# Column scans that keep the running line in contiguous buffers and let ScalarE copy it home, with the rows written out in four strips

## The chip, the cores and the metric

One core of a Trainium2 chip. The metric is the device time of one execution in microseconds (us); times of several runs are given as their median. Profiled values come from one execution of the program. The engines are TensorE (PE in the rows, PEld for its weight loads), VectorE (DVE), ScalarE (ACT), GpSimd (POOL) and SyncE (SP), which here only issues transfers.

## The reference

The input is `x` of shape (4, 48, 128, 128) in float32. Four residual layers are applied to it, each to a group-normalised copy:

```python
x = x + _L0_conv_ref(_gn(x), ...)   # 1x1 and 3x3 convolutions, channel attention
x = x + _L1_conv_ref(_gn(x), ...)   # four line scans
x = x + _L2_conv_ref(_gn(x), ...)   # the same with other weights
x = x + _L3_conv_ref(_gn(x), ...)   # gated MLP over tokens
```

A scan layer walks over the image line by line. Every new line is the old content of that line plus a 5-tap convolution of the line that was finished just before, over 48 channels in and out:

```python
def f(carry, inp):
    nxt = inp + _conv1d(carry, w, b)
    return (nxt, nxt)
```

It does so over the rows downwards, over the rows upwards, over the columns to the right and over the columns to the left, 127 steps each. No step can start before the one before it is done. Eight such scans (two layers of four) stand in the program.

## The kernel before

The whole image stays on the chip in `image`, in float32. The 128 partitions hold two halves: 48 channels from partition 0 (`LO`) and 48 from partition 64 (`HI`), for even and odd positions along the line, so that the 5 taps become three products of 112 x 112 weights. The free dimension is `(g s k j b)`: `g` a pair of the four batches and `b` the batch in it, `s` and `k` the row or column index (`s` its parity), `j` the position along a row. `line(g, along_w, at)` gives one line of two batches, 128 numbers in a partition. In a row scan these are one contiguous run of 512 bytes. In a column scan (`along_w`) they are 64 pairs of numbers: 8 bytes each, 512 bytes from one to the next.

One scan step runs the two groups g = 0 and 1 in turn. TensorE makes three products into `bank[g]` (lines 1134 to 1136; each is two instructions with a weight load each), counted by `s_prod[g]`. VectorE adds the old line to the bank and writes the new line into `image` (line 1489), counted by `s_state[g]`, on which TensorE's next step of that group waits. While VectorE adds for one group, TensorE multiplies for the other. In the program's numbering the scans are 0 (down), 1 (up), 2 (right) and 3 (left); `SCANS` holds them, and 2 and 3 are the column scans.

Around the scans:

- During scan 1 ScalarE exchanges the halves of finished rows (`exchange`, three copies for every two steps, in a loop of its own), so that the column scans find their layout. It does nothing in scan 2.
- The layer's input is kept in HBM (`saved`) as 16 tiles, four to each strip of 16 column indices `j` (32 columns). SyncE brings them into six buffers (`bring`) and, in the first scan layer, saves the sums again.
- In scan 3, whenever a half strip (16 columns) is finished, GpSimd adds the kept input to it in the buffer (`add_strips`, four adds for a half strip, waiting for `s_prod`). ScalarE then copies the sums back into `image` (`swap_home` in the first layer, `rows_home` in the second, 8 instructions for a half strip) and counts `s_home`. VectorE takes statistics of what came home (`strip_piece`), one instruction behind each add. There are eight half strips; the last is added by VectorE itself (`add_last`) when the scan has ended.
- In the second scan layer SyncE also writes the finished rows to HBM (`send_rows`, in two halves of the row, for four batches) and reads them back as tokens (`bring_tokens`) for the MLP. `s_flat[b]` counts the rows of batch b. GpSimd and ScalarE wait for `s_flat[1]`, since two of the MLP's buffers lie where batch 1 stood, and TensorE waits for GpSimd's four fills of these buffers (`s_gate_zero`) before it turns the first tokens.

An instruction of these engines carries one wait with it. Where the program puts two waits ahead of an instruction, the instruction carries the first one and the second becomes an instruction of its own that runs ahead of it.

## Time and profile before

| | us |
|---|---|
| median of 3 runs | 2387.31 (2385.31 to 2390.0) |
| the profiled execution | 2381.65 |
| its span, first to last instruction | 2379.8 |
| mean granted clock of TensorE | 0.971 of full speed |

The profiled execution lies 5.66 us under the median of the runs. Its scans stand between 740 and 2140 us of the span: the first layer's from 743 to 1427 us, the second's from 1455 to 2140 us. Before them are the convolutions and the attention, behind them the MLP. A row of the timeline has start and duration in us, engine, line, operation and shapes, and in brackets the idle time ahead of it with what ended it.

### The profile page before, as it was taken

The page shows a single profiled execution, that of the slowest core. Times are in us where ns is not written, and L with a number is a line of the kernel's source. Part 1 is how long each engine was busy: PE and PEld are TensorE (multiplying, and loading weights), DVE is VectorE, ACT ScalarE, POOL GpSimd, SP SyncE. Part 2 cuts the span into 40 slices and gives each one's busy share as a digit, 9 for nine tenths or more (in the row PEclk, how much of TensorE's full clock was granted, in tenths as well). Part 3 has the DMA queues.
Part 4 walks back from the last instruction along what each step waited for, and adds up shares of the span by engine and source line. Part 5 has one row for each costly group of instructions (what it writes and reads, how often), then busy time and mean ns, then how long its engine had stood idle before and what let it go on. Part 6 is the DMA issues. An engine that isn't in the chain of part 4 may idle for free.

```text
span 2379.8 us, 42935 instructions
## 1 busy us (share of the span) xinstructions
PE 2182.0 (92%) x17386; PEld 1969.6 (83%) x17386; DVE 1396.8 (59%) x3514; ACT 761.6 (32%) x1088; POOL 412.7 (17%) x411
## 2 busy tenths in 40 slices
PE   2989999999999999999999995999999999992786
PEld 2889759669536999999999995999999999991554
DVE  5866666766775444444555886444444555884555
ACT  6922342442546002440002347003440001223542
POOL 2233203213104800000003430300000003430200
PEclk9999999999999999999999997999999999996998
DMA  7700111121237940000001531400000000567835
GB/s 128 117 12 11 13 25 16 15 45 37 55 57 145 145 89 2 1 1 1 1 1 40 148 108 54 81 1 2 1 1 1 1 1 18 102 122 202 275 107 159
DMA packets 237974, 139.31 MB, mean 59 GB/s; under 512 B 197728, under 2 KB 222560, under 8 KB 230368
## 3 DMA queue, kind: packets, MB, share of 16 engines
q1 hardware_dynamic: 236640, 135.79, 27.0%
q8 instruction: 136, 2.23, 0.4%
q10 hardware_dynamic: 1024, 0.91, 0.2%
q14 instruction: 46, 0.38, 0.1%
q0 software_dynamic: 128, 0.01, 0.0%
HBM read 77.06 MB, written 62.92 MB: 59 GB/s over the span
## 4 chain that ended last, share of the span: by engine, by line
PE 87%; DVE 7%; ACT 2%; DMA 1%; issue 1%; SPq 1%; POOL 0%; ACTq 0%; DVEq 0%; POOLq 0%
PE bank L1134 20%; PE bank L1135 19%; PE bank L1136 18%; PE bank L1024 10%; PE bank L1095 7%; PE bank L1027 4%; PE bank L1098 2%; DVE work L1412 2%; PE bank L1246 2%; PE bank L1039 1%; PE bank L1173 1%; PE bank L1218 1%; DVE stats L1269 1%; DMA image<-flat_rows 1%; SPq L577 1%
## 5 line engine op out<-in xcount | busy, mean ns | idle before, releaser
L1489 DVE TENSOR_TENSOR image<-bank,image 112x128 f32<-112x128 f32 x2032 | 656.5, 323 | 638.8 <-PE bank L1136 609.3
L1134 PE MATMUL bank<-image,scan_area 112*112 112x128 f32 x4064 | 807.3, 280 | 12.8 <-ACT image L875 6.7
L1135 PE MATMUL bank<-image,scan_area 112*112 112x126 f32 x4064 | 771.2, 271 | 0.0
L1136 PE MATMUL bank<-image,scan_area 112*112 112x126 f32 x4064 | 770.2, 270 | 0.0
L1135 PEld LDWEIGHTS bank<-image,scan_area 112*112 112x112 f32 x4064 | 581.6, 176 | 0.0
L1134 PEld LDWEIGHTS bank<-image,scan_area 112*112 112x112 f32 x4064 | 567.1, 175 | 16.5 <-ACT image L875 7.1
L1136 PEld LDWEIGHTS bank<-image,scan_area 112*112 112x112 f32 x4064 | 578.9, 176 | 0.0
L1024 PE MATMUL bank<-work 128*128 128x192 f32 x1536 | 307.5, 337 | 28.6 <-DVE work L1412 27.2
L372 POOL TENSOR_TENSOR work<-image,work 112x1024 f32<-112x1024 f32 x56 | 129.2, 2337 | 1078.2 <-PE bank L1136 1076.3
L1024 PEld LDWEIGHTS bank<-work 128*128 128x128 f32 x1536 | 249.5, 194 | 34.2 <-issue 33.1
L807 ACT COPY work<-work 32x1008 f32<-32x1008 f32 x128 | 132.0, 1031 | 297.8 <-PE bank L1027 194.7
L1412 DVE COPY work<-work 32x1008 f32<-32x1008 f32 x256 | 208.7, 815 | 4.5
L667 POOL TENSOR_TENSOR band<-band,work 128x384 f32<-128x384 f32 x124 | 145.8, 1176 | 285.2 <-DVE work L1370 285.2
L871 ACT COPY work<-image 48x256 f32 (+1 forms) x128 | 51.5, 403 | 418.1 <-PE bank L1136 417.8
L1095 PE MATMUL bank<-work 128*48 128x512 f32 x768 | 179.7, 602 | 4.0 <-DVE work L1404 4.0
L881 ACT COPY image<-work 48x1024 f32<-48x1024 f32 x64 | 67.1, 1049 | 292.7 <-POOL work L372 282.6
L1027 PE MATMUL bank<-work 96*128 96x96 f32 x1024 | 151.1, 270 | 0.0
L1027 PEld LDWEIGHTS bank<-work 96*128 96x128 f32 x1024 | 150.4, 194 | 0.0
L1095 PEld LDWEIGHTS bank<-work 128*48 128x48 f32 x768 | 51.6, 124 | 115.7 <-issue 111.1
L1367 DVE COPY work<-bank 128x384 f32<-128x384 f32 x128 | 71.3, 557 | 128.2 <-PE bank L1027 126.9
L890 ACT ACTIVATE image<-work,b_col 112x512 f32<-112x512 f32 x64 | 44.7, 777 | 313.6 <-POOL work L372 302.7
L799 ACT ACTIVATE work<-image,gn_shift,gn_scale 112x576 f32<-112x576 f32 (+1 forms) x128 | 110.7, 908 | 2.3 <-DVE gn_shift L1311 0.9
(163 smaller groups left out, 1524.0 us busy)
## 6 DMA issues: line engine op xcount, KB each, us to landing
work<-saved SPq DMA_DIRECT2D x64, 384.0 KB, 8.5
saved<-saved SPq DMA_DIRECT2D x32, 384.0 KB, 7.4
saved<-work SPq DMA_DIRECT2D x32, 384.0 KB, 5.7
flat_rows<-image SPq DMA_DIRECT2D x16, 768.0 KB, 13.1
image<-flat_rows SPq DMA_DIRECT2D x4, 3072.0 KB, 18.1
out<-image SPq DMA_DIRECT2D x8, 1536.0 KB, 7.1
work<-work SPq DMA_DIRECT2D x128, 70.9 KB, 2.8
band<-in_x SPq DMA_DIRECT2D x16, 384.0 KB, 5.9
```

The lines of the kernel that those rows point to most:

```text
L372: return vector.tensor_tensor(dst, in_image(g, w, half, slice(0, P)), dst, ALU.add)
L667: nc.gpsimd.tensor_tensor(norm_sum[b % 2], norm_sum[b % 2], square[i % 2], ALU.add)\
L799: last = nc.scalar.activation(dst.rearrange("p (k j) -> p k j", j=J2), src, ACT.Identity, bias=gn_shift[0:P, b:b + 1], scale=gn_scale[0:P, ...
L807: last = nc.scalar.copy(packed(g % 2, 1, side), quarter(g % Z_BUFS, 1, side))
L1024: mm(dst, blk_z[g % Z_BUFS][:, o:o + 2 * J2], qk_w[:, dy], start=(dy == 0), stop=False)
L1027: last = mm(dst.rearrange("p (t s c) -> p t s c", t=2, s=2)[:, :, side, :], blk_2[g % 2][:, side, sub, o:o + 2 * J2], qk_w2[:, side, :].re ...
L1095: mm(bank_out[sub][cols, :], out_w_sides[:, dy, side, :], blk_z[g % Z_BUFS][:, o:o + BLK * J2], start=(dy == 0), stop=False)
L1134: mm(dst, wt[:, 1], src, start=True, stop=False)
L1135: mm(dst[:, 1:J2, :], wt[:, 0], src[:, 0:J2 - 1, :], start=False, stop=False)
L1136: mm(dst[:, 0:J2 - 1, :], wt[:, 2], src[:, 1:J2, :], start=False, stop=True).then_inc(s_prod[g], 1)
L1412: last = v.tensor_copy(packed(g % 2, dy, side), quarter(g % Z_BUFS, dy, side))
L1489: v.tensor_tensor(line(g, along_w, at), prod, line(g, along_w, src), ALU.add).then_inc(s_state[g], 1)
```

## The change

In the column scans VectorE no longer writes the new line into `image`, but into one of two contiguous buffers `fresh` (256 numbers in a partition, both groups; step i uses buffer i mod 2). TensorE reads its next line from there. ScalarE copies both groups' line from the buffer into `image` with one instruction a step and counts `s_line`: in scan 2 in a loop of two steps a turn, in scan 3 written out. VectorE's add of group 0 waits, besides for TensorE, for the copy of two steps ago; the wait for TensorE stands first.

The copies home of a half strip are no longer made at once: one of their eight instructions follows every second line copy, beginning 6 steps and a half strip later (`HOME_AT`). GpSimd's adds wait for `s_line` instead of `s_prod`. VectorE's `add_last` waits for the last line copy.

The rows of the second layer go out by strips: `send_rows` takes 16 column indices instead of 32, so pieces of 128 bytes instead of 256, in 32 transfers instead of 16, and the first three strips go out during scan 3. Behind the last strip's rows of batch 0 stands `bring_tokens(0)`, and only then the rows of batch 1.

```diff
+HOME_AT = 6
+LINES = 2 * (H - 1)
...
+        band_pair = sb("band_pair", [128, 256])
+        band_tmp = [band_pair[:, 0:128], band_pair[:, 128:256]]
+        fresh = [v[0:P, 0:256].rearrange("p (g n) -> p g n", g=2) for v in (stats, band_pair)]
...
-            def send_rows(half, b):
+            def send_rows(strip, b):
-                j = J2 - (half + 1) * 2 * STRIP
+                j = J2 - (strip + 1) * STRIP
                 for h, rows in enumerate((LO, HI)):
-                    sp.dma_start(lines[h, b, :, :, 2 * j:2 * j + 4 * STRIP],
-                                 image_l[rows, b // 2, b % 2, :, j:j + 2 * STRIP, :].rearrange("p k j b -> p k (j b)"))\
+                    sp.dma_start(lines[h, b, :, :, 2 * j:2 * (j + STRIP)],
+                                 image_l[rows, b // 2, b % 2, :, j:j + STRIP, :].rearrange("p k j b -> p k (j b)"))\
                         .then_inc(s_flat[b], 16)
...
                     for t in (4 * strip + 2 * g, 4 * strip + 2 * g + 1):
                         if t + GAP < TILES:
                             bring(t + GAP)
-                    if strip == 1:
-                        send_rows(0, 2 * g)
-                        send_rows(0, 2 * g + 1)
+                    send_rows(strip, 2 * g)
+                    send_rows(strip, 2 * g + 1)
             sp.wait_ge(s_home, 2 * HOMES - 1)
-            send_rows(1, 0)
-            send_rows(1, 1)
+            send_rows(STRIPS - 1, 0)
             bring_tokens(0)
+            send_rows(STRIPS - 1, 1)
             sp.wait_ge(s_home, 2 * HOMES)
-            send_rows(1, 2)
+            send_rows(STRIPS - 1, 2)
             bring_tokens(1)
-            send_rows(1, 3)
+            send_rows(STRIPS - 1, 3)
...
-                        pool.wait_ge(s_prod[g], (layer * PASSES + 3) * STEPS + 2 * HALF_STRIP * (half + 1))
+                        pool.wait_ge(s_line, layer * LINES + STEPS + 2 * HALF_STRIP * (half + 1) - 1)
...
-                for half in range(LAST + 1):
+                state0 = layer * (PASSES * STEPS + 1) + 2 * STEPS + 1
+                with act.Fori(0, K2 - 1) as i:
+                    for m in range(2):
+                        for g in range(2):
+                            own_wait(act, s_state[g], 2 * i + (state0 + m + 1))
+                        nc.scalar.copy(both_lines(((m + 1) % 2, i + (m + 1) // 2)),
+                                       fresh[m].rearrange("p g (k b) -> p g k b", b=2)).then_inc(s_line, 1)
+
+                for n in range(STEPS - 1, LINES):
                     for g in range(2):
-                        if half < LAST:
-                            act.wait_ge(s_kept_p, layer * 4 * LAST + 4 * half + 2 * g + 2)
-                        else:
-                            act.wait_ge(s_kept_v, layer * 4 + 2 * g + 2)
-                        (rows_home if layer else swap_home)(g, half).then_inc(s_home, 1)
+                        act.wait_ge(s_state[g], state0 + n + 1)
+                    at = n + 1 if n < STEPS else LINES - 1 - n
+                    nc.scalar.copy(both_lines((at % 2, at // 2)),
+                                   fresh[n % 2].rearrange("p g (k b) -> p g k b", b=2)).then_inc(s_line, 1)
+                    half, part = divmod(n - STEPS - HOME_AT, 2 * HALF_STRIP)
+                    if half > 0 and part % 2 == 0:
+                        home_parts(layer, half - 1, part // 2, part // 2 + 1)
+                done = (STEPS - 1 - HOME_AT) % (2 * HALF_STRIP) // 2 + 1
+                home_parts(layer, LAST - 1, done, 8)
+                home_parts(layer, LAST, 0, 8)
...
+                    if along_w and (scan, n) != (2, 0):
+                        src = fresh[(done - 1) % 2][:, g, :].rearrange("p (j b) -> p j b", b=2)
...
+                i = done - 2 * STEPS
+                if i == 0:
+                    dve.wait_ge(s_band, N_BAND + layer * (G + 1))
                 for g in range(2):
                     dve.wait_ge(s_prod[g], done + (layer * PASSES * STEPS + 1))
+                    if g == 0 and i >= 2:
+                        dve.wait_ge(s_line, layer * LINES + i - 1)
-                    v.tensor_tensor(line(g, along_w, at), prod, line(g, along_w, src), ALU.add).then_inc(s_state[g], 1)
+                    dst = line(g, along_w, at)
+                    if along_w:
+                        dst = fresh[done % 2][:, g, :].rearrange("p (j b) -> p j b", b=2)
+                    v.tensor_tensor(dst, prod, line(g, along_w, src), ALU.add).then_inc(s_state[g], 1)
...
             def add_last(layer):
 
+                dve.wait_ge(s_line, (layer + 1) * LINES)
                 for g in range(2):
-                    dve.wait_ge(s_state[g], (layer + 1) * PASSES * STEPS + layer + 1)
```

`home_parts` waits for GpSimd's (or VectorE's) adds ahead of each group's four copies, and makes the copies that `swap_home` and `rows_home` made:

```python
def home_parts(layer, half, first, end):
    for n in range(first, end):
        g, part = n // 4, n % 4
        if part == 0 and half < LAST:
            act.wait_ge(s_kept_p, layer * 4 * LAST + 4 * half + 2 * g + 2)
        elif part == 0:
            act.wait_ge(s_kept_v, layer * 4 + 2 * g + 2)
        last = home_part(layer, g, half, part)
        if part == 3:
            last.then_inc(s_home, 1)
```

## Rows read from the trace of the kernel before

**Rows 1.** The page: the chain by engine, and GpSimd's adds of the kept input.
```profile
PE 87%; DVE 7%; ACT 2%; DMA 1%; issue 1%; SPq 1%; POOL 0%; ACTq 0%; DVEq 0%; POOLq 0%
...
L372 POOL TENSOR_TENSOR work<-image,work 112x1024 f32<-112x1024 f32 x56 | 129.2, 2337 | 1078.2 <-PE bank L1136 1076.3
```

**Rows 2.** Windows of line 1489, one scan each: length, busy time (count), granted clock.
```profile
911.30:1075.80 164.50, 74.10 (x254) 1.00 0.01 1
1080.10:1254.00 173.90, 89.72 (x254) 0.99 0.01 1
1254.20:1427.50 173.30, 90.41 (x254) 1.00 0.37 101
...
1791.00:1966.20 175.20, 89.78 (x254) 0.99 0.01 1
1966.40:2139.70 173.30, 90.24 (x254) 1.00 0.44 83
```

**Rows 3.** Timeline of a row scan: two adds, and weight loads of the product behind each.
```profile
1000.21 0.29 DVE L1489 TENSOR_TENSOR image<-bank,image 112x128 f32<-112x128 f32 x1 [0.36 <-PE bank L1136]
1000.86 0.29 DVE L1489 TENSOR_TENSOR image<-bank,image 112x128 f32<-112x128 f32 x1 [0.36 <-PE bank L1136]
...
1000.55 0.28 PEld L1134 LDWEIGHTS bank<-image,scan_area 112*112 112x112 f32 x2
```

**Rows 4.** Timeline of column scans: adds, weight loads, a copy home, the scan's last add.
```profile
1182.68 0.36 DVE L1489 TENSOR_TENSOR image<-bank,image 112x128 f32<-112x128 f32 x1 [0.35 <-PE bank L1136]
1183.33 0.29 DVE L1489 TENSOR_TENSOR image<-bank,image 112x128 f32<-112x128 f32 x1 [0.29 <-PE bank L1136]
...
1183.09 0.27 PEld L1134 LDWEIGHTS bank<-image,scan_area 112*112 112x112 f32 x2
...
1183.73 0.28 PEld L1134 LDWEIGHTS bank<-image,scan_area 112*112 112x112 f32 x2
...
1416.27 1.05 ACT L881 COPY image<-work 48x1024 f32<-48x1024 f32 x1 [1.42 <-POOL work L372]
...
1416.88 0.29 DVE L1489 TENSOR_TENSOR image<-bank,image 112x128 f32<-112x128 f32 x1
...
1427.20 0.29 DVE L1489 TENSOR_TENSOR image<-bank,image 112x128 f32<-112x128 f32 x1 [0.33 <-PE bank L1136]
```

**Rows 5.** Timeline of a row scan: an add whose wait for TensorE stands second.
```profile
765.38 0.29 DVE L1489 TENSOR_TENSOR image<-bank,image 112x128 f32<-112x128 f32 x1 [0.42 <-PE bank L1136]
```

**Rows 6.** Groups of ScalarE's instructions by shape: busy us, mean ns, idle before.
```profile
L881 ACT COPY image<-work 48x1024 f32<-48x1024 f32 x64 | 67.1, 1049 | 292.7 <-POOL work L372 282.6 <-DVE work L372 9.5
...
L871 ACT COPY work<-image 48x256 f32 x124 | 49.9, 403 | 417.8 <-PE bank L1136 417.8
```

**Rows 7.** Timeline of SyncE's queue: the time in which the transfers are issued.
```profile
747.56 85.19 SPq L545 DMA_DIRECT2D saved<-saved  x32
...
2061.82 20.81 SPq L577 DMA_DIRECT2D flat_rows<-image  x4
2082.68 7.14 SPq L553 DMA_DIRECT2D work<-saved  x4
...
2145.16 16.84 SPq L577 DMA_DIRECT2D flat_rows<-image  x4
```

**Rows 8.** Timeline and chain from the last scan's end to the first tokens.
```profile
2139.86 4.63 DVE L372 TENSOR_TENSOR work<-image,work 112x1024 f32<-112x1024 f32 x4 [0.19 <-DVE image L1489]
...
2142.26 5.43 ACT L890 ACTIVATE image<-work,b_col 112x512 f32<-112x512 f32 x8 [10.89 <-DVE work L372]
...
2162.10 17.74 DMA image<-flat_rows
...
2169.20 0.98 POOL L738 MEMSET work<- 32x512 f32 x2 [20.49 <-DMA flat_rows<-image]
2170.13 0.99 POOL L738 MEMSET image<- 32x512 f32 x2
...
2181.43 2.87 PE L1173 MATMUL bank<-identp,image 128*96 128x128 f32 x12 [18.66 <-DVE image L1584]
```

More of the change, by code:

```diff
@@ L230, in build @@
         gam_sb, bet_sb, dwb_sb, pwb_sb, pwr_sb = (gates[:, 72 + 8 * i:80 + 8 * i] for i in range(5))
-        band_tmp = [sb(f"band_tmp{i}", [128, 128])[:, :] for i in range(2)]
+        band_pair = sb("band_pair", [128, 256])
+        band_tmp = [band_pair[:, 0:128], band_pair[:, 128:256]]
         pick = band_tmp[0][:, 0:WQ]
+        fresh = [v[0:P, 0:256].rearrange("p (g n) -> p g n", g=2) for v in (stats, band_pair)]
         w2r_sb = sb("w2r_sb", [128, TOK])
@@ L289, in build @@
         s_swap = sem("s_swap")
+        s_line = sem("s_line")
         s_ready = sem("s_ready")
@@ L735, in _ @@
             pool.wait_ge(s_gn, 6)
[L736 removed]
+            pool.wait_ge(s_flat[1], 32 * STRIPS)
             for m in range(4):
@@ L875, in exchange, with home_part, both_lines @@
                 nc.scalar.copy(part(HI, 0), swap_tmp[HI]).then_inc(s_swap, 1)
-            def swap_home(g, half):
-                for w, to in enumerate((LO, HI)):
-                    for h, of in enumerate((LO, HI)):
-                        last = nc.scalar.copy(in_image(g, h, half, to), in_buffer(g, w, half, of))
-                return last
-            def rows_home(g, half):
-                for b in range(2):
-                    for w in range(2):
-                        dst = in_image(g, b, half, slice(0, P)).rearrange("p k (j w) -> p w k j", w=2)
-                        src = in_buffer(g, w, half, slice(0, P)).rearrange("p k (j b) -> p b k j", b=2)
-                        last = nc.scalar.activation(dst[:, w], src[:, b], ACT.Identity, bias=b2_col[0:P, :], scale=1.0)
-                return last
+            def home_part(layer, g, half, part):
+                a, c = part // 2, part % 2
+                if layer == 0:
+                    return nc.scalar.copy(in_image(g, c, half, (LO, HI)[a]), in_buffer(g, a, half, (LO, HI)[c]))
+                dst = in_image(g, a, half, slice(0, P)).rearrange("p k (j w) -> p w k j", w=2)
+                src = in_buffer(g, c, half, slice(0, P)).rearrange("p k (j b) -> p b k j", b=2)
+                return nc.scalar.activation(dst[:, c], src[:, a], ACT.Identity, bias=b2_col[0:P, :], scale=1.0)
+            def home_parts(layer, half, first, end):
+                for n in range(first, end):
+                    g, part = n // 4, n % 4
+                    if part == 0 and half < LAST:
+                        act.wait_ge(s_kept_p, layer * 4 * LAST + 4 * half + 2 * g + 2)
+                    elif part == 0:
+                        act.wait_ge(s_kept_v, layer * 4 + 2 * g + 2)
+                    last = home_part(layer, g, half, part)
+                    if part == 3:
+                        last.then_inc(s_home, 1)
+            def both_lines(at):
+                s, j = at
+                return image_l[:, :, s, :, ds(j, 1), :].rearrange("p g k j b -> p g (k j) b")
             for layer in range(2):
```

5 lines of the change are left out of this document (2 added, 3 removed).

## The prediction

> **What bounds the kernel now.** I read the page first. TensorE carries 87% of the chain [rows 1], but that alone doesn't say whether it is at its own limit. So I went to the eight scans, cut the trace into one window each, and compared row scans with column scans [rows 2]. Each has the same 254 adds and the same products, yet a row scan takes 164.5 us and a column scan 173.3 to 175.2. Per step of two groups that is 164.5 / 127 = 1.295 us against 1.365. The adds differ too: 74.1 / 254 = 0.292 us against 90.4 / 254 = 0.356.
>
> The timeline shows how the one makes the other. In a row scan an add ends 0.05 us before the weight load of its group's next product, 1000.50 against 1000.55 [rows 3]. In a column scan it is the same 0.05 us, 1183.04 against 1183.09, but the add took 0.36; where an add took 0.29, the load came 0.11 us after its end, at TensorE's own pace [rows 4]. So in row scans the add just fits behind the other group's products, and 0.064 us more in each add lengthen the step by 0.069. Column scans are bound by the loop TensorE, VectorE, TensorE; row scans stand at the point where the two limits meet.
>
> Why is the add longer? Not by its strides alone: the last add of a scan, with TensorE idle, has the same strides and takes 0.29, and so does every eighth add while TensorE works [rows 4]. In these eighth adds the column that TensorE reads and the column that VectorE works on lie in different aligned 16-byte places of the 512-byte row; in the other seven they share the place. My reading is that two strided streams meet in the same part of the memory and VectorE pays. Copies by ScalarE elsewhere in `image` don't matter: the add at 1416.88 takes 0.29 in the middle of one [rows 4].
>
> **The change, step by step.** The sum is made against the profiled execution, 2381.65 us, which is 5.66 us below the median of the runs; I add the 5.66 at the end.
>
> Adds and products: TensorE reads contiguous buffers in all but the first step, and VectorE writes them; only VectorE's read of the old line stays strided. The two streams that met are gone, so I take the row scan's length for each column scan. Four scans at 173.3 - 164.5 = 8.8 give **-35.2 us**. (The two that begin with a lower clock are 0.6 and 1.9 us longer [rows 2]; I leave that with them.) The bounds are 0, if the strided read alone keeps the add at 0.356, and -35.2.
>
> The Trainium skill speaks against this term. Its Vector Engine (DVE) Microarchitecture Reference, section 5.2 Measured stream behaviour on trn2, says that streams in pairs of adjacent words on 8-byte boundaries run at full rate whatever the hop between pairs. The last add of the scan agrees, at 0.29 [rows 4]. By that rule alone the layout costs nothing and the term would be 0; the rows with TensorE at work say otherwise.
>
> The second wait: where the wait for TensorE stands second, the add starts after 0.42 us of idling instead of 0.36 [rows 5, 3], so 0.06 us later. Here it stands first and is carried by the add; the wait for `s_line` runs ahead of it, while VectorE idles 0.35 us anyway [rows 4] or is busy with statistics. Cost 0 as long as the copy of two steps ago is done then. That copy can start about 0.1 us after its step's second add (0.3 in the loop, with address arithmetic) and takes 0.40 for 256 numbers [rows 6], so it is done within 0.7 us, some 0.9 us early. In scan 3 a home copy of 1.05 us [rows 6] can stand ahead of every other line copy; that still leaves about 0.8 us. ScalarE's load is 2 x 0.40 + 1.05 = 1.85 us in two steps of 2.59. Queued behind a late wait would be the add, then the products, so each late us would count. The first step of each scan 2 has the wait for TensorE second: 2 x 0.06 = **+0.1**.
>
> Line copies meeting adds: ScalarE writes pairs with a hop of 512 bytes, and the next add of group 0 reads a neighbouring column, in three of four steps in the same 16-byte place. No row shows such a copy against an add. Lower bound 0, as for the copy at 1416.88. Upper bound the price that TensorE's reads cost, 0.064 us on one add a step: 508 x 3/4 x 0.064 = 24.4. The copy overlaps the add's reading in part, and the add no longer writes there; I take **+3**.
>
> Home copies and GpSimd: GpSimd's four adds of a half strip take 2.34 us each [rows 1] and are started about where they are now. The first home copy comes 8 steps later, 10.4 us, for two adds of 4.7; it blocks ScalarE, and with it the line copies, only if a tile comes about 4 steps late. VectorE's statistics wait for the fourth home copy two steps behind it: 0.94 for that step's adds, 0.1, 0.40 and 1.05 make 2.5 of 2.9 us. Cost 0; if the cover goes, 24 such waits at 0.3 us, 7 us. At the first layer's end VectorE's last adds wait for the line copy, 0.1 + 0.40: **+0.5**.
>
> Rows out: before, four transfers of 3072 pieces of 256 bytes took 20.8 us in SyncE's queue, 5.2 each [rows 7]. Now there are 32 with as many pieces of 128 bytes. The nearest row is the transfer from HBM to HBM with 3072 pieces of 128 bytes, 85.19 / 32 = 2.66 us [rows 7]. The price r of one is between 2.66 (bytes decide) and 5.2 (pieces decide); I take 3.3, near the first, since size and count are its own, and above it, since 48 partitions of the chip's memory are the source. From the home copies of the first strip (about step 46) to the end of the scan are 80 x 1.295 + 0.9 = 104.5 us. In them the queue has 20 transfers of tiles at 7.14 / 4 = 1.8 [rows 7] and 24 of rows: 36 + 24 r. The excess over 104.5 stands ahead of the last strip: 10.7 us at 3.3, none below 2.85. Then come two transfers (batch 0), the tokens (10.6 us: they landed at 2179.84, the rows ahead of them at 2169.2), two transfers (batch 1), and GpSimd's fills, 1.9 [rows 8], for which TensorE waits: 10.7 + 6.6 + 10.6 + 6.6 + 1.9 = 36.4 us after the last add, against 2181.43 - 2139.67 = 41.8 now [rows 8]. That gains 5.4; as SyncE must see batch 0's rows land before it issues the tokens, I take **-4**. At 2.66 the last home copy, about 6.2 us after the last add, is what counts, and the gain is at most 12.5. At 5.2 it is 56 + 10.4 + 10.6 + 10.4 + 1.9 = 89.3, a loss of 47.5. Break-even is near r = 3.5.
>
> The Trainium skill has a price for this. DMA: Bandwidth & Descriptors, Why small descriptors are slow, gives a packet 32 bytes a cycle and about 3 cycles on top: 11 cycles for 256 bytes, 7 for 128. From the row's 5.2 us an estimate by that page is r = 3.3 and the same gain; no row here shows 128-byte pieces out of the chip's memory.
>
> **Sum.** -35.2 + 0.1 + 3 + 0.5 - 4 = -35.6: the profiled execution at 2346.0 us, the median at **2351.7, say 2352**.
>
> **The rivals.**
>
> *ScalarE's line copies take TensorE's place* in the conflict: adds of group 0 stay at about 0.35 in three of four steps. For it: the place is shared as before, and only one side changed. Against it: the overlap is short, and just one add a step is hit, though one is enough for the loop. Up to 24.4 instead of 3: 2373.
>
> *The rows in small pieces become the bound*, the one that ends on the other side. It has its place in SyncE's queue during the last scan: the same 3072 pieces a transfer, twice the transfers. If pieces decide, the first tokens come 47.5 us later instead of 4 earlier: 2403. It decides from 28 r = 97.8 + 31.6, r = 4.6 (31.6 is what the other terms leave to be lost). For it: 5.2 us for a transfer whose bytes at the HBM-to-HBM row's rate need the same 5.3 us, which leaves open which of the two decides; against it: 2.66 us for as many pieces [rows 7]. Between r = 3.6 and 4.5 lies a smaller gain, 2358 to 2384.
>
> *The adds stay long*: the strided read is kept, and if it is the read that suffers under any work of TensorE, the loop stays at 1.365 and the time at 2387. Against it: the 0.29 us of every eighth add, with TensorE at work.
>
> **Chances and range.** Forecast 0.60; line copies 0.15; rows at a middle price 0.08; rows at the full price 0.10; adds stay long 0.07. What differs by less than 0.2%, 4.8 us, can't be told from no change in this kernel. Faster: 0.60 + 0.15 + 0.07 + 0.01 = 0.83; the same: 0.01 + 0.04 = 0.05; slower: 0.10 + 0.02 = 0.12. The range goes from 2342 (r near 2.7, no conflict) to 2382, which leaves out the full price and most of the long adds. The forecast's own range is 2342 to 2359.
>
> **What would show it.** Right: adds at 0.29 in all column scans, windows of 164 to 167 us, the weight load at 0.11 us or at the row scan's 0.05 after the add; no wait of VectorE for ScalarE; 32 transfers of rows at about 3.3 us; TensorE's first tokens 32 to 40 us after the last add. Wrong: adds of group 0 at 0.33 to 0.36 with every fourth step short; ScalarE idle for GpSimd while VectorE waits for `s_line`; SyncE still issuing the third strip's rows when the last half strip is home.

## The result and the profile after

| | before | after |
|---|---|---|
| median of 4 runs, us | 2386.31 (2383.91 to 2390.0) | 2345.0 (2339.15 to 2347.66) |
| the profiled execution, us | 2381.65 | 2339.15 |
| its span, us | 2379.8 | 2337.3 |
| last add to TensorE's first tokens, us | 41.8 | 34.7 |

The ratio is 0.9822, with a 95% interval from 0.9804 to 0.9839: 41 us faster. Forecast were 2352 in a range from 2342 to 2382.

First the adds of the column scans, cut into one window for each scan, as in [rows 2]. Columns: the window, its length, VectorE's busy time in these adds, and the rest as there. The line of the add is now 1526.

```profile
1079.00:1244.36 165.36, 74.96 (x254) 0.99 0.01 1
1244.70:1409.04 164.34, 74.24 (x254) 1.00 0.42 107
1773.00:1939.49 166.49, 74.94 (x254) 0.99 0.01 1
1939.80:2104.17 164.37, 74.27 (x254) 1.00 0.61 98
```

The two scans 3 (second and fourth line) have the row scan's length now, and its adds of 0.292 us (74.24 / 254). The two scans 2 are 1.0 and 2.1 us longer, with adds of 0.295 in the mean; they begin 4.7 us after the last add of scan 1, and TensorE's mean granted clock is 0.81 in the first 5 us of the one and 0.79 in the first 10 us of the other, then 1.00. Against [rows 2] the four are 8.5, 9.0, 8.7 and 8.9 us shorter, 35.1 together.

The groups of the adds and of the line copies by shape (busy us, mean ns of one, idle time ahead and what ended it):

```profile
L1526 DVE TENSOR_TENSOR image<-bank,image 112x128 f32<-112x128 f32 x1016 | 296.5, 292 | 369.4 <-PE bank L1165 369.4
L1526 DVE TENSOR_TENSOR stats<-bank,image 112x128 f32<-112x128 f32 x508 | 149.5, 294 | 151.5 <-PE bank L1165 150.5
L1526 DVE TENSOR_TENSOR band_pair<-bank,image 112x128 f32<-112x128 f32 x508 | 148.9, 293 | 143.6 <-PE bank L1165 140.0
L936 ACT COPY image<-band_pair 112x256 f32 x126 | 57.3, 455 | 111.9 <-DVE band_pair L1526 111.9
L943 ACT COPY image<-band_pair 112x256 f32<-112x256 f32 x128 | 54.7, 427 | 101.5 <-DVE band_pair L1526 101.5
```

The first group is the row scans, the next two are the column scans: VectorE's idle time is nearly all TensorE's, not ScalarE's. Of the 508 adds of group 0 in the column scans none waits last for ScalarE. A line copy takes 0.43 to 0.46 us.

Then the end. SyncE's queue in scan 3 of the second layer, for [rows 7]:

```profile
1999.04 1.70 SPq L558 DMA_DIRECT2D work<-saved  x4
2000.79 16.69 SPq L582 DMA_DIRECT2D flat_rows<-image  x4
...
2022.03 15.33 SPq L582 DMA_DIRECT2D flat_rows<-image  x4
2040.55 2.27 SPq L558 DMA_DIRECT2D work<-saved  x4
...
2063.10 16.04 SPq L582 DMA_DIRECT2D flat_rows<-image  x4
2082.03 1.70 SPq L558 DMA_DIRECT2D work<-saved  x4
2083.78 34.18 SPq L582 DMA_DIRECT2D flat_rows<-image  x10
```

And the chain behind the last add, which ends at 2104.2, for [rows 8]:

```profile
2104.26 0.41 ACT image L943
2104.66 8.07 ACT image L888 x12
2112.73 2.21 SPq L582
...
2114.99 7.04 DMA flat_rows<-image
...
2123.08 13.62 DMA flat_rows<-image
...
2136.84 0.98 POOL work L742 x2
2137.82 0.94 POOL image L742 x2
...
2138.85 1.27 PE bank L1202 x5
```

The last strip's rows are issued from 7.7 us after the last add on (2111.89), because the queue is busy with the third strip until then. (The chain puts ScalarE's twelve copies ahead of them, which end at 2112.73. But the rows of batch 0 wait only for the eighth, which ends at 2110.10; the queue ends the third strip at 2111.84.) TensorE waits last for GpSimd's fills (2136.84), these for the rows of batch 1 (2123.08 + 13.62), and those stand behind the tokens of batch 0.

Of the 42.5 us between the two profiled executions, 35.1 lie in the column scans, 7.1 in the stretch behind them, 1.3 ahead of the first scan, where nothing was changed; the joint between the layers is 0.6 longer (28.4 us from the last add to the next scan's first, against 27.9) and the other joints 0.4. From the first tokens to the end, in the MLP, it took 198.5 us, as before (198.4). In the profiles of the experiments this stretch takes from 198.5 to 204.2, and the granted clock differs with it: 0.94 in a stretch of 150 us of it here, 0.92 in about the same stretch of a second profile of the same kernel, where the MLP took 203.7. So parts are compared by their own stretches.

### The profile page after: what moved, and what is told of

It is laid out like the page before. It is cut to its first block, busy times and chain, and to the rows that moved or that the text cites. A ratio compares the mean times of both kernels' runs of the same rounds, so it can differ in the third digit from the quotient of the medians.

```text
span 2337.3 us, 45480 instructions
## 1 busy us (share of the span) xinstructions
PE 2146.9 (92%) x17386; PEld 1936.7 (83%) x17386; DVE 1336.1 (57%) x3514; ACT 980.9 (42%) x1596; POOL 414.6 (18%) x411
## 4 chain that ended last, share of the span: by engine, by line
PE 87%; DVE 7%; ACT 2%; DMA 2%; issue 1%; POOL 0%; SPq 0%; ACTq 0%; DVEq 0%; POOLq 0%
PE bank L1163 19%; PE bank L1164 19%; PE bank L1165 19%; PE bank L1051 10%; PE bank L1122 7%; PE bank L1054 4%; PE bank L1125 2%; DVE work L1441 2%; PE bank L1275 2%; PE bank L1066 1%; PE bank L1202 1%; PE bank L1247 1%; DMA flat_rows<-image 1%; DVE stats L1298 1%; DMA band<-in_x 1%
## 5 line engine op out<-in xcount | busy, mean ns | idle before, releaser
L1526 DVE TENSOR_TENSOR image<-bank,image 112x128 f32<-112x128 f32 x1016 | 296.5, 292 | 369.4 <-PE bank L1165 369.4
L1163 PE MATMUL bank<-image,scan_area 112*112 112x128 f32 x2040 | 392.0, 274 | 12.7 <-ACT image L879 6.7
L1164 PE MATMUL bank<-image,scan_area 112*112 112x126 f32 x2040 | 388.5, 272 | 0.0
L1165 PE MATMUL bank<-image,scan_area 112*112 112x126 f32 x2040 | 388.0, 271 | 0.0
L1163 PEld LDWEIGHTS bank<-image,scan_area 112*112 112x112 f32 x2040 | 289.0, 176 | 14.4 <-ACT image L879 7.1
L1164 PEld LDWEIGHTS bank<-image,scan_area 112*112 112x112 f32 x2040 | 293.5, 178 | 0.0
L1165 PEld LDWEIGHTS bank<-image,scan_area 112*112 112x112 f32 x2040 | 292.5, 178 | 0.0
L1526 DVE TENSOR_TENSOR stats<-bank,image 112x128 f32<-112x128 f32 x508 | 149.5, 294 | 151.5 <-PE bank L1165 150.5
L1526 DVE TENSOR_TENSOR band_pair<-bank,image 112x128 f32<-112x128 f32 x508 | 148.9, 293 | 143.6 <-PE bank L1165 140.0
L1163 PE MATMUL bank<-stats,scan_area 112*112 112x128 f32 x1016 | 194.0, 272 | 0.0
L1164 PE MATMUL bank<-stats,scan_area 112*112 112x126 f32 x1016 | 193.0, 272 | 0.0
L1165 PE MATMUL bank<-stats,scan_area 112*112 112x126 f32 x1016 | 192.6, 270 | 0.0
L1163 PE MATMUL bank<-band_pair,scan_area 112*112 112x128 f32 x1008 | 192.0, 272 | 0.0
L1164 PE MATMUL bank<-band_pair,scan_area 112*112 112x126 f32 x1008 | 190.9, 271 | 0.0
L1165 PE MATMUL bank<-band_pair,scan_area 112*112 112x126 f32 x1008 | 190.5, 270 | 0.0
```

What stands on the lines that cost most here:

```text
L1163: mm(dst, wt[:, 1], src, start=True, stop=False)
L1164: mm(dst[:, 1:J2, :], wt[:, 0], src[:, 0:J2 - 1, :], start=False, stop=False)
L1165: mm(dst[:, 0:J2 - 1, :], wt[:, 2], src[:, 1:J2, :], start=False, stop=True).then_inc(s_prod[g], 1)
L1526: v.tensor_tensor(dst, prod, line(g, along_w, src), ALU.add).then_inc(s_state[g], 1)
```

## The experiments

Two tell the parts of the change apart, two the cause of the long adds, the others the waits and transfers. The times:

| run | median us | ratio, 95% interval | last add to first tokens |
|---|---|---|---|
| rows as before | 2355.7 | 0.9876 [0.9859, 0.9892] | 46.9 |
| rows alone | 2376.1 | 0.9965 [0.9951, 0.9978] | 30.6 |
| other place | 2361.8 | 0.9905 [0.9890, 0.9921] | 42.1 |
| one side | 2353.1 | 0.9870 [0.9854, 0.9887] | 41.9 |
| the change again | 2347.5 | 0.9840 [0.9827, 0.9853] | 36.2 |
| rows first | 2343.8 | 0.9830 [0.9816, 0.9844] | 34.5 |
| home early | 2339.2 | 0.9812 [0.9796, 0.9828] | 32.9 |
| both | 2341.3 | 0.9820 [0.9806, 0.9833] | 31.3 |
| wait second | 2375.0 | 0.9962 [0.9952, 0.9972] | 34.1 |
| last copy | 2419.2 | 1.0151 [1.0131, 1.0171] | 33.9 |
| small pieces | 2390.9 | 1.0028 [1.0015, 1.0041] | 72.1 |
| home by fours | 2390.7 | 1.0021 [1.0009, 1.0033] | 31.0 |

**Which two streams meet: another place for TensorE's column.** In the kernel before:

```diff
-                    src = line(g, along_w, at)
+                    read = at
+                    if along_w:
+                        d = 8 if layer else 4
+                        if not forward:
+                            d = -d
+                        read = at + d if 0 <= at + d < H else at - d
+                    src = line(g, along_w, read)
```

> The kernel before, but in the column scans TensorE reads, still strided, a column further on in the scan's direction: 4 columns (16 bytes) in the first scan layer, 8 columns (32 bytes) in the second. The recurrence of the column scans is therefore not computed; all instructions, shapes and waits stay. The theory, that an add is long when TensorE's column and VectorE's column share an aligned place of 16 bytes of the 512: in the first layer the pattern turns over, and now only every eighth add (group 0 in one step of four) shares the place and takes 0.356 us, the other seven 0.292; each of these scans has about 32 steps that are 0.069 us longer, so 166 to 167 us. In the second layer no add shares it: 0.292 throughout, 164 us. In all about 31 us faster: 2356, a ratio of 0.987. The rival that any strided read by TensorE lengthens VectorE's strided add: 0.356 everywhere, 173 us, ratio 1.000. A rival that goes by distance and not by aligned places: no long adds in the first layer either, 164 us in all four, ratio 0.985.

The windows of its four column scans, and the timeline of VectorE in the first layer:

```profile
1080.20:1248.94 168.74, 76.30 (x254) 0.99 0.00 1
1249.20:1416.95 167.75, 76.43 (x254) 1.00 0.37 105
1780.70:1948.85 168.15, 74.11 (x254) 0.99 0.01 1
1949.10:2115.01 165.91, 74.11 (x254) 1.00 0.46 87
```

```profile
1159.42 0.35 DVE L1495 TENSOR_TENSOR image<-bank,image 112x128 f32<-112x128 f32 x1 [0.36 <-PE bank L1142]
1160.08 0.29 DVE L1495 TENSOR_TENSOR image<-bank,image 112x128 f32<-112x128 f32 x1 [0.30 <-PE bank L1142]
1160.78 0.29 DVE L1495 TENSOR_TENSOR image<-bank,image 112x128 f32<-112x128 f32 x1 [0.41 <-PE bank L1142]
...
1164.05 0.29 DVE L1495 TENSOR_TENSOR image<-bank,image 112x128 f32<-112x128 f32 x1 [0.36 <-PE bank L1142]
1164.70 0.36 DVE L1495 TENSOR_TENSOR image<-bank,image 112x128 f32<-112x128 f32 x1 [0.36 <-PE bank L1142]
...
1169.98 0.36 DVE L1495 TENSOR_TENSOR image<-bank,image 112x128 f32<-112x128 f32 x1 [0.36 <-PE bank L1142]
```

The adds came as the theory had it, the time did not: the four scans are 25 us shorter and not 31, and the median is 2361.8 us against 2356. The pattern turned over. With TensorE 16 bytes further on, the adds at 1159.42, 1164.70 and 1169.98, every eighth, are the long ones, and the seven between them are short; in [rows 4] it was the reverse. With 32 bytes no add is long (74.11 / 254 = 0.292), though both engines go through strided columns as before. Distance alone is ruled out (columns 8 bytes apart occur in two steps of four, and only the one within an aligned place is slow), and so is "any strided read". What remains of the length seems to be TensorE's own: short adds follow each other every 0.653 us here and every 0.648 in a row scan, which makes 165.9 us of a scan instead of 164.4. In four scans that is the 6 us that are missing. The next run tells whose it is.

**Which side pays.** In the kernel before, VectorE's write is moved to a contiguous buffer in the first layer, and TensorE's read in the second:

```diff
+                    dst = line(g, along_w, at)
+                    if along_w and layer == 0:
+                        dst = fresh[:, g, :].rearrange("p (j b) -> p j b", b=2)
-                    v.tensor_tensor(line(g, along_w, at), prod, line(g, along_w, src), ALU.add).then_inc(s_state[g], 1)
+                    v.tensor_tensor(dst, prod, line(g, along_w, src), ALU.add).then_inc(s_state[g], 1)
...
                     src = line(g, along_w, at)
+                    if along_w and layer == 1:
+                        src = fresh[:, g, :].rearrange("p (j b) -> p j b", b=2)
```

> The kernel before with one side of the meeting changed in each layer. First layer: in the column scans VectorE writes into a contiguous buffer and still reads the old line strided, while TensorE reads its strided column in the image (which is not updated, so the recurrence is not computed). Second layer: TensorE reads a fixed contiguous buffer, while VectorE reads and writes its strided column (the recurrence is not computed here either). The theory that two strided streams must meet: the second layer's adds take 0.292 us and its column scans 164 us, with VectorE as strided as before. In the first layer the theory leaves open which of VectorE's two streams pays: if it is the read, the adds stay at 0.356 and the scans at 173; if the write, 0.292 and 164. In all 17.6 us faster (2369, ratio 0.993) or 35 (2352, ratio 0.985). The rival that VectorE's strided streams are slow whenever TensorE works: 0.356 in the second layer, and if the write is the slow one 0.292 in the first, ratio 0.993 too, but with the layers the other way round; with the read as the slow one 1.000.

Its windows:

```profile
1081.50:1248.56 167.06, 75.05 (x254) 0.99 0.01 1
1248.80:1414.79 165.99, 75.27 (x254) 1.00 0.38 106
1778.50:1945.40 166.90, 74.16 (x254) 0.99 0.01 1
1945.70:2110.07 164.37, 74.17 (x254) 1.00 0.47 88
```

Second layer: 0.292 us and 164.4, with VectorE as strided as ever. First layer: 75.27 / 254 = 0.296, so of the 0.064 us the strided write paid 0.060 and the read 0.004. As far as the adds go, either half alone takes the long ones away. The 1.5 us are TensorE's strided read: the last scan takes 166.0 in the first layer, where TensorE still reads strided, and 164.4 in the second, where it doesn't and VectorE does. The median, 2353.1, is near the 2352 expected if the write pays.

**The two parts apart.** The change with the old rows (the diff), and the kernel before with the new ones (the same edit the other way round):

```diff
-                j = J2 - (strip + 1) * STRIP
+                j = J2 - (half + 1) * 2 * STRIP
...
-                    send_rows(strip, 2 * g)
-                    send_rows(strip, 2 * g + 1)
+                    if strip == 1:
+                        send_rows(0, 2 * g)
+                        send_rows(0, 2 * g + 1)
...
-            send_rows(STRIPS - 1, 0)
-            bring_tokens(0)
-            send_rows(STRIPS - 1, 1)
+            send_rows(1, 0)
+            send_rows(1, 1)
+            bring_tokens(0)
```

> The change with the rows written out as before it: two halves of the row in pieces of 256 bytes, 16 transfers, the tokens of batch 0 behind all rows of the first two batches. The theory: the change is made of two parts that don't touch each other. The column scans keep what they gained (lengths of 164 to 166 us, adds of 0.292 us), and the stretch from the last add to TensorE's first tokens goes back from 34.7 us to about 41.8. So about 7 us above the changed kernel: 2352 for the median, a ratio to the kernel before of 0.985. The rival: the rows' 24 transfers that now run during scan 3 cost nothing and gain nothing, and the end got shorter for another reason (home copies that come one by one): then the stretch stays at 34.7 us and the ratio at 0.982.

> The kernel before with nothing but the rows of the change: four strips, pieces of 128 bytes, 32 transfers, the tokens of batch 0 ahead of the rows of batch 1. The theory of two separate parts: the column scans stay at 173 to 175 us with adds of 0.356, and the stretch from the last add to TensorE's first tokens falls from 41.8 us to about 34.7, so 7 us faster: 2380, a ratio of 0.997. The forecast had 4 us for this part, 0.998. The rival, that pieces decide a transfer's time (5.2 us each as with 256 bytes), gives a loss of some 40 us, 1.018; a rival that the scans have to be shorter first for the rows to gain gives 1.000.

The rows alone gave 11.1 us in this stretch, not 7: first tokens 30.6 us after the last add (the median fell by 7.7). The change without the new rows lost 5.2 there: 46.9. The scans were as expected in both (164.3 and 173.1 us in the last one). So the parts do touch each other, and something in the column scans' part costs the end 4 to 5 us. SyncE's queue in the run with the rows alone, where the last add ends at 2141.1, shows it:

```profile
2063.21 15.56 SPq L577 DMA_DIRECT2D flat_rows<-image  x4
2078.82 4.53 SPq L553 DMA_DIRECT2D work<-saved  x4
...
2105.30 1.70 SPq L553 DMA_DIRECT2D work<-saved  x4
2107.05 43.00 SPq L577 DMA_DIRECT2D flat_rows<-image  x10
```

The third strip comes home 36 us before the last add (2105.30); in the change it is 22 us (2082.03 against 2104.2). What delays it in the change should be that the copies home are handed out one by one; the runs after the next tell. With the old rows, this delays the tiles as well: GpSimd's last add before the end begins at 2109.66, 2.8 us after the last add of the scan, for want of a tile.

**The copies home sooner, and the rows of batch 1 ahead of the tokens.** The first edit below is the run "home early", the second "rows first", the two together "both"; run beside the change itself:

```diff
-HOME_AT = 6
+HOME_AT = 3
...
             send_rows(STRIPS - 1, 0)
-            bring_tokens(0)
             send_rows(STRIPS - 1, 1)
+            bring_tokens(0)
```

> The changed kernel itself, unaltered, so that the next three can be held against it on one chip: about 2345, a ratio to the kernel before of 0.982, and 34.7 us from the last add to TensorE's first tokens.

> The changed kernel with its copies home three steps sooner (HOME_AT 3 instead of 6). The theory: handing the copies home out one by one delays the rows. With the rows alone changed, the third strip's rows were all issued 5 us before the last add and TensorE's first tokens came 30.6 us after it; in the change they were issued until 7.7 us after it and the tokens came at 34.7. Three steps are 3.9 us; the queue then is through with the third strip at about 4 us after the last add, and the last strip's first copies home (about 6 us) decide: 1.7 to 3.9 us gained, first tokens at 31 to 33 us, 2341 to 2343, ratio 0.981. VectorE and the scans stay as they are, since GpSimd's two adds of 4.7 us are done in the 5 steps of 6.5 us that are left. One rival: the place of the copies home costs nothing, as the forecast had it: 34.7 us and 2345. Another: ScalarE now waits for GpSimd with line copies behind it, and the scan 3 windows grow by up to 24 waits of 0.3 us, 7 us.

> The changed kernel with the last strip's rows of batch 1 ahead of the tokens of batch 0, as the order was before the change. The theory: TensorE's first tokens wait last for GpSimd's fills, the fills for the rows of batch 1, and these stand behind the tokens in SyncE's queue, so the new order of the change costs time. Four transfers of 3.05 us from 7.7 us after the last add are issued by 19.9 and landed by 24, the fills end at 26; the tokens, issued behind, need some 10 us and land at 30, and VectorE's first third of the normalising adds 1.3: TensorE starts at about 31.3 us instead of 34.7, so 3.4 us faster than the change, 2342, ratio 0.981. The rival, that the order is right because the tokens are the longer way: the tokens come later by the two transfers, 6 us, TensorE starts at 36 to 38 us and the kernel is 2 to 3 us slower than the change.

> The changed kernel with both edits: the copies home three steps sooner and the rows of batch 1 ahead of the tokens. If the two causes stand one behind the other, as the theory has it, the gains add: first tokens 28 to 30 us after the last add, 5 to 6 us faster than the change, 2339 to 2340, ratio 0.980. If only one wait counts, it is no better than the better of the two alone.

Home early: first tokens after 32.9 us, against 34.7 and 36.2 in the two profiles of the change, and the scans unchanged (164.3 in the last one); that is 1.8 to 3.3 us, within the 1.7 to 3.9 expected. The queue explains it: the first transfer of the last strip is issued 6.0 us after the last add, against 7.7 and 9.1, and from there to the first tokens it is 26.9 us here, 27.0 and 27.1 there. Its median is 8.3 us below the change's, but the rest of that lies in stages that the edit doesn't touch (the MLP 200.4 us against 203.7), so only these 2 to 3 us are shown to be its own. No other median is lower, though it isn't clear of that of "both".

Rows first: neither expectation held. TensorE starts at 34.5 us, against 34.7 and 36.2 in the change. From its timeline:

```profile
2124.83 2.93 SPq L589 DMA_DIRECT2D image<-flat_rows  x1
...
2129.95 0.98 POOL L742 MEMSET work<- 32x512 f32 x2 [15.69 <-DVE tok_shift L1329]
...
2137.69 3.86 DVE L1621 TENSOR_SCALAR image<-image,gn_scale,tok_shift 128x2048 f32<-128x2048 f32 x3 [7.85 <-DMA image<-flat_rows]
```

The fills came 7 us sooner, as the theory had it, but the tokens land at 2137.6, 32.9 us after the last add instead of 28: the wait changed its name. Both edits together give 31.3, which is 1.6 better than the home copies alone, too little to show in the medians; 28 to 30 were expected, and here too TensorE waits last for the tokens.

**Handing out against bundles.**

```diff
-                    if half > 0 and part % 2 == 0:
-                        home_parts(layer, half - 1, part // 2, part // 2 + 1)
-                done = (STEPS - 1 - HOME_AT) % (2 * HALF_STRIP) // 2 + 1
-                home_parts(layer, LAST - 1, done, 8)
+                    if half > 0 and part % 8 == 0:
+                        home_parts(layer, half - 1, part // 2, part // 2 + 4)
```

> The changed kernel with the copies home in bundles of four, one group of a half strip at a time, instead of one behind every second line copy; the first of each bundle keeps its place. The theory, that handing them out is what keeps the line copies in time: in the first layer a bundle takes 4 x 1.05 = 4.2 us behind a line copy, the next line copy ends 5.2 us after its step's last add where it should be read at 3.0, so VectorE loses 2.2 us at each of 14 bundles, 31 us; in the second layer the copies take 0.77, it loses 1.1 us each, 15 us. The last strips come home sooner and give back up to 4 us at the end. In all 40 to 46 us slower than the change, ratio about 1.00. The rival, that the buffers' slack swallows the bundles: ratio 0.981 to 0.983.

Its two windows of scan 3:

```profile
1249.80:1455.88 206.08, 73.96 (x254) 0.93 0.32 85
1986.30:2158.83 172.53, 73.88 (x254) 1.00 0.62 100
```

From the first add to the end of the last, scan 3 took 206.0 us in the first layer (+41.7, 3.0 for each bundle) and 172.4 in the second (+8.1, 0.6 each): 50 us in all against 46 expected, unevenly. VectorE waited last for ScalarE 13 times in each, for 30.8 us in the first and 10.5 in the second: about what the theory had (31 and 15). In the first layer's scan 3 the mean granted clock is 0.93 where it is 1.00 in the change's, so part of the rest may be the clock's; no run separates it. The end came 3.7 us sooner (31.0). So handing out pays for itself many times over, at 3.7 us.

This also settles what the delay at the end was. With the bundles the third strip comes home 29.8 us before the last add instead of 22.1, the queue is through with it by then, and the last strip's rows are issued 5.9 us after the last add, as soon as they are home; with the rows alone at 5.4. From there to the first tokens it is 25.1 and 25.2 us in these two runs, against 27 in the three where the queue was still full.

**The order of the two waits.**

```diff
                 for g in range(2):
-                    dve.wait_ge(s_prod[g], done + (layer * PASSES * STEPS + 1))
                     if g == 0 and i >= 2:
                         dve.wait_ge(s_line, layer * LINES + i - 1)
+                    dve.wait_ge(s_prod[g], done + (layer * PASSES * STEPS + 1))
```

> The changed kernel with the two waits of group 0's add in the other order: the wait for the line copy first, so that the add carries it, and the wait for TensorE second, as an instruction of its own ahead of the add. The theory: the add of group 0 then starts 0.06 us later after its products, as in the row scans' first step, and each such delay counts, because in the run with the other place a group 0 add that was 0.064 us longer made its step 0.06 us longer. 126 steps of four scans at 0.06 are 30 us: 2375, a ratio of 0.995, column scans of about 171.5 us with adds still at 0.292. The rival: the order costs nothing, since VectorE idles 0.36 us there: 164 us, ratio 0.983.

As expected: 27 to 30 us above the change's two medians, with adds as short as ever. In the trace the wait for TensorE is now an instruction of its own, 0.06 us ahead of the add. Its windows in the first layer:

```profile
1081.20:1254.23 173.03, 74.14 (x254) 0.99 0.01 1
1254.60:1427.29 172.69, 74.11 (x254) 1.00 0.39 102
```

A step of scan 3 takes 1.359 us instead of 1.294 (the scan's length from add to add, over 127), 0.065 more; in scan 2, once under way, 1.357 instead of 1.297, 0.060 more. Of the 508 adds of group 0 only 21 wait last for ScalarE, so it isn't the copies that are late. The order of two lines of the program is worth most of the gain.

**How early the line copies are.** The add of group 0 waits for the copy of the step just before:

```diff
-                    if g == 0 and i >= 2:
-                        dve.wait_ge(s_line, layer * LINES + i - 1)
+                    if g == 0 and i >= 1:
+                        dve.wait_ge(s_line, layer * LINES + i)
```

> The changed kernel with the add of group 0 waiting for the line copy of the step just before it instead of the one before that, as a single buffer would want it. The theory, that the copies are done some 0.9 us ahead of need and that only two buffers make this so: the copy starts 0.1 us (0.3 in the loop) after its step's second add and takes 0.44, the next add of group 0 could start 0.36 after that same add, so it comes 0.2 to 0.4 us late, in some 500 steps, and in the first layer's scan 3 a copy home of 1.05 us adds to every second one: 100 to 200 us slower than the change, a ratio to the kernel before of 1.03 to 1.07, with scan 3 longer in the first layer than in the second. The rival, that TensorE's products hide the copy: ratio 0.983.

74 us slower than the change's first median, less than expected: scan 2 takes 188.0 and 187.5 us (0.17 to 0.18 more a step), scan 3 179.9 and 179.7 (0.12), and the first layer's longer copies home don't show. The wait is real and two buffers are needed, but my size for it was too large by a factor of about two. VectorE's timeline in scan 2 of the first layer shows why:

```profile
1160.61 0.57 DVE L1526 TENSOR_TENSOR stats<-bank,image 112x128 f32<-112x128 f32 x2 [0.73 <-ACT image L936]
1161.90 0.29 DVE L1526 TENSOR_TENSOR band_pair<-bank,image 112x128 f32<-112x128 f32 x1 [0.72 <-PE bank L1165]
1162.55 0.29 DVE L1526 TENSOR_TENSOR band_pair<-bank,image 112x128 f32<-112x128 f32 x1 [0.36 <-PE bank L1165]
1163.56 0.57 DVE L1526 TENSOR_TENSOR stats<-bank,image 112x128 f32<-112x128 f32 x2 [0.73 <-ACT image L936]
```

Only every second step waits for the copy. After such a wait both groups' products lie ready and the two adds run back to back (x2). The second add, and the copy behind it, so come sooner, and the copy is done before the next products are: the step behind a late one is on time. Steps of 1.67 and 1.29 us alternate. In all four column scans 274 of the 508 adds of group 0 wait last for ScalarE. One late step costs the 0.2 to 0.4 us that were expected, and about half of the steps are late. In the change itself, with two buffers, each copy ends about 1.0 us before the add that waits for it starts in scan 2, and at least 0.67 before it in scan 3.

**What a piece costs.** Three strips in pieces of 64 bytes:

```diff
-                    sp.dma_start(lines[h, b, :, :, 2 * j:2 * (j + STRIP)],
+                    size = HALF_STRIP if strip < STRIPS - 1 else STRIP
+                    for at in range(j, j + STRIP, size):
+                        sp.dma_start(lines[h, b, :, :, 2 * at:2 * (at + size)],
...
```

> The changed kernel with the rows of the first three strips in pieces of 64 bytes instead of 128, 48 transfers instead of 24, each again of 3072 pieces; the last strip stays at 128. It measures what a piece and what a byte costs. From 5.2 us for 256 bytes and 3.05 for 128 a straight line gives 0.9 us and 2.15 us for each 128 bytes, so 1.97 us for 64: 48 transfers need 95 us instead of 73, the queue is 22 us later with the third strip, and the whole some 20 us slower than the change, 2365, ratio 0.992. The rival, that at this size pieces decide and not bytes, gives 2.7 to 3.05 us again, 56 to 73 us more, ratio 1.007 to 1.014.

```profile
2001.11 1.70 SPq L558 DMA_DIRECT2D work<-saved  x4
2002.85 24.21 SPq L584 DMA_DIRECT2D flat_rows<-image  x8
2027.10 3.98 SPq L558 DMA_DIRECT2D work<-saved  x4
```

From 2001.11 to 2027.10 are 26.0 us; less 7.1 for the four tiles [rows 7] that leaves 2.36 for each of the eight; in steady stretches one follows the other every 2.41 us. So 5.2 us for 256 bytes, 3.05 for 128, 2.4 for 64: halving the pieces again buys little, and neither the straight line (1.97) nor the rival (2.7 to 3.05) was right. The run was some 45 us slower than the change, where 20 or 56 and more were expected. By the prediction's reckoning the queue had 48 x 2.4 + 36 = 151 us of work in the 104.5 us behind the first strip's copies home. The tiles came late, GpSimd waited 20.5 us for them, and scan 3 grew to 172.6 us; the first tokens came 72.1 us after the last add. That is the rival of the rows as the bound, brought about by more pieces.

## Why the prediction was right, point by point

**The bound and the cause.** That the column scans were bound by the loop of TensorE and VectorE and the row scans stand where the limits meet is borne out: every 0.06 us on an add counted, whether it came from the memory (other place) or from a wait (wait second). The reading of the aligned 16-byte places was an inference from every eighth add; it is now shown, by the pattern that turned over. (The 0.356 us of the prediction is the mean over a scan, short adds included; the long ones alone take 0.365.) What I had not seen is that nearly all of it is VectorE's write, and that 1.5 of the 8.8 us a scan are TensorE's own strided read.

**Adds and products**: -35.2 forecast, -35.1 measured.

The Trainium skill's Vector Engine (DVE) Microarchitecture Reference, section 5.2 Measured stream behaviour on trn2, lets pairs of adjacent words on 8-byte boundaries hop at no cost. The run with TensorE 32 bytes further on agrees: 0.292 us with both of VectorE's streams strided. Where TensorE read the same 16-byte place, the adds with a strided write took 0.06 us more in the mean of a scan, and by that rule it would be nothing; the measurement decides.

**The second wait and the layer's end**: +0.1 and +0.5 forecast. The joint between the layers is 0.6 longer: the last adds begin 0.72 us after the scan's instead of 0.19. The joints ahead of the scans 2, where the +0.1 belongs, are 0.2 longer together. The price of 0.06 us for a wait that stands second is confirmed at 0.060 to 0.065 by the run that turned the order.

**Line copies meeting adds**: +3 forecast, 0 measured. This term was mis-sized. In scan 2 the adds of group 0 do take 298 ns instead of 292, at most 309, but the steps stay at 0.648 us a group. The rival that ScalarE takes TensorE's place fell with it.

**Home copies and GpSimd**: 0 forecast. In the scans that is right: VectorE's waits are TensorE's. But the handing out put the third strip's rows 13.7 us nearer to the end (36 us before it with the rows alone, 22 in the change), and that cost 3.7 us of the end (home by fours) to 4.1 (34.7 against 30.6 with the rows alone). The forecast had the late start inside its 104.5 us for the rows, without seeing that this was a price of the home copies.

**Rows out**: -4 forecast, -7.1 measured. The price r was 3.05 instead of 3.3 (the length of one transfer in the steady stretch ahead of 2111.89) and came between the bounds. With it the formula gives 4.7 + 6.1 + 10.6 + 6.1 + 1.9 = 29.4 us. It left out that the queue waits for copies home ahead of the second and of the third strip: from 2037.36 to 2040.55 and from 2079.14 to 2082.03, 6.1 us of idling. With these 35.5, against 34.7. That this comes so near is in part luck: the queue was through with the third strip 7.7 us after the last add and not 4.7 + 6.1 = 10.8, and from there it took 27.0 us and not 24.7. The prediction had also named, as a sign of being wrong, that the queue still issues the third strip's rows when the last half strip is home. For the half of it that batch 0's rows wait for, this came true by 1.7 us (2111.84 against 2110.10); for all of it, it didn't (2112.72). The sign was ill chosen, since the prediction's own sum had the queue 10.7 us behind. That the tokens stand ahead of batch 1's rows and TensorE ends up waiting for the fills came as forecast.

The Trainium skill's DMA: Bandwidth & Descriptors, Why small descriptors are slow, counts 11 cycles for 256 bytes; by its rule 128 and 64 bytes take 7 and 5, which makes estimates of 3.3 and 2.36 us from the 5.2 of 256 bytes. The runs show 3.05 and 2.40: the estimates are right within a tenth.

**The sum.** 2352 against 2345.0: 3 us are the line copies, 3 the rows, and 1.3 lie ahead of the scans, less some tenths in the joints.

What stays open: what exactly in the memory the shared 16-byte place is; the runs show when the price falls due, not the mechanism. Open too is how much of the first layer's loss with the bundles is the clock's.

## What to carry to other kernels

Where two engines take turns in one step, compare the same instruction in a stage where it is fast and one where it is slow, and look for the period of the exceptions: every eighth short add held the cause, and a shift of the address by 16 and by 32 bytes showed it in one run. In such a loop let the instruction carry the wait that comes last: the wrong order cost 0.060 to 0.065 us a step, two thirds of the gain. When copies are handed out to keep one queue short, follow the queue that waits for them: here the rows' transfers paid 4 us of the 11 that they had gained.

## What the runs showed of the hardware that was not expected

- An add of VectorE with a strided write takes 0.365 us instead of 0.292 for 128 numbers in a partition while TensorE reads, strided too, in the same aligned 16 bytes of the 512-byte row (0.356 in the mean of a scan, where one add in eight is short); in the neighbouring 16 bytes 0.292. VectorE's strided read there costs 0.004.
- TensorE's strided reads make the three products of one group 0.653 us instead of 0.648.
- A wait that is an instruction of its own ahead of the add, and ends last, makes a step 0.060 to 0.065 us longer than one that the add carries.
- 3072 pieces of this pattern out of the chip's memory take about 5.2, 3.05 and 2.4 us with 256, 128 and 64 bytes each.
